# Picking table rows inside the edge loop of a graph layer: from three tiles of one group to one tile of most groups

## The reference

```
row, col = src, dst
h   = relu(bn(concat(x[row], edge_attr) @ W1 + b1))      # 53125 x 128, bn over all edges
agg = segment_sum(h, col) / max(count(col), 1)           # 3125 x 128
h2  = relu(bn(concat(x, agg) @ W2 + b2))                 # 3125 x 256, bn over all nodes
out = layernorm(x + relu(h2 @ Wl + bl))                  # 3125 x 128
```

## Time and profile before

| | us |
|---|---|
| time, three runs | 586.23, 587.31, 763.84 (median 587.31) |
| profiled execution, its own time | 585.97 |
| its span, first to last instruction | 584.2 |
| PE busy | 527.9 (90%) |
| PE weight loads busy | 464.9 (80%) |
| DVE busy | 509.0 (87%) |
| ACT busy | 425.3 (73%) |
| POOL busy | 362.0 (62%) |

### The profile page before, as it was taken

One profiled execution on the slowest core, in us unless ns is written; L12 is line 12 of the kernel. 1 busy time (PEld: TensorE's weight loads), 2 busy tenths in 40 slices (PEclk: granted clock), 3 DMA queues, 4 the chain that ended last, 5 costly groups with the idle time before them and its releaser, 6 DMA issues.

```text
span 584.2 us, 10621 instructions
## 1 busy us (share of the span) xinstructions
PE 527.9 (90%) x3099; PEld 464.9 (80%) x3099; DVE 509.0 (87%) x719; ACT 425.3 (73%) x850; POOL 362.0 (62%) x464
## 2 busy tenths in 40 slices
PE   3679999999999999999999988898997999999993
PEld 4658878877778878888888877787885999999583
DVE  5796999999999999999999989898986877777787
ACT  2458777887788777888888877678767566666476
POOL 4776777777777777777777777777770333333500
PEclk9789999999999999999999999899999999999997
DMA  7844454455444554444444444354345688775004
GB/s 197 263 142 125 158 161 143 133 162 167 155 140 146 163 166 141 140 145 139 143 145 148 145 150 148 109 148 150 95 121 164 219 252 267 251 253 169 1 1 111
DMA packets 48139, 90.21 MB, mean 154 GB/s; under 512 B 10885, under 2 KB 30260, under 8 KB 48099
## 3 DMA queue, kind: packets, MB, share of 16 engines
q1 hardware_dynamic: 30734, 59.97, 31.2%
q0 software_dynamic: 10912, 22.37, 15.0%
q10 hardware_dynamic: 6453, 7.38, 3.6%
HBM read 66.71 MB, written 22.97 MB: 153 GB/s over the span
## 4 chain that ended last, share of the span: by engine, by line
PE 55%; DVE 20%; issue 8%; POOL 8%; ACT 4%; DMA 3%; DVEq 0%; ACTq 0%; POOLq 0%
PE psT L784 22%; PE psH L923 8%; PE psC L923 8%; POOL res L682 6%; DVE node_hot L1319 6%; PE psH L766 5%; PE psT L847 4%; DVE psX L1334 3%; PE psC L766 2%; DVE res L1306 2%; PE psH L793 1%; DMA res<-ytab,srci 1%; DVE res L1473 1%; POOL res L666 1%; ACT node_rows_turned L1084 1%
## 5 line engine op out<-in xcount | busy, mean ns | idle before, releaser
L682 POOL DMA_INDIRECT res<-ytab,srci x265 | 250.2, 944 | 81.8 <-issue 77.1
L784 PE MATMUL psT<-node_hot,node_table 125*128 125x384 f32 x1250 | 261.9, 358 | 4.5 <-DVE node_hot L1319 3.7
L784 PEld LDWEIGHTS psT<-node_hot,node_table 125*128 125x128 f32 x1250 | 222.3, 191 | 29.5 <-issue 12.5
L1319 DVE TENSOR_TENSOR node_hot<-agg,psC 125x1920 fp32r<-125x1920 int32 x75 | 161.0, 2147 | 0.0
L1094 ACT ACTIVATE node_hot<-agg,nodeid 125x384 fp32r<-125x384 int32 x250 | 131.8, 603 | 8.8 <-PE psT L784 6.6
L1097 ACT ACTIVATE node_hot<-node_hot,ones 125x1920 fp32r<-125x1920 f32 x50 | 95.1, 1902 | 1.6
L1435 DVE TENSOR_TENSOR work<-res,psX 128x512 f32<-128x512 f32 x104 | 70.8, 687 | 20.2 <-PE psH L923 10.1
L707 POOL TENSOR_TENSOR agg<-agg,srci 128x64 f32 x104 | 32.0, 308 | 74.6 <-ACT srci L1161 55.0
L766 PE MATMUL psH<-w1e,work 128*128 128x256 f32 x268 | 70.5, 385 | 6.0 <-DVE res L1304 3.3
L682 POOL DMA_INDIRECT work<-ytab,srci x64 | 60.7, 948 | 23.7 <-issue 16.8
L1334 DVE TENSOR_TENSOR psX<-agg,psX 128x512 f32<-128x512 f32 x103 | 71.1, 690 | 4.4 <-ACT agg L1031 4.3
(11 more groups left out here) (222 smaller groups left out, 534.8 us busy)
## 6 DMA issues: line engine op xcount, KB each, us to landing
work<-in_edge_attr SPq DMA_DIRECT2D x26, 512.0 KB, 3.6
res<-spill SPq DMA_DIRECT2D x25, 512.0 KB, 3.6
spill<-work SPq DMA_DIRECT2D x13, 512.0 KB, 2.8
spill<-res SPq DMA_DIRECT2D x12, 512.0 KB, 2.9
agg<-in_src_rows SPq DMA_DIRECT2D x25, 192.0 KB, 3.9
res<-ytab,srci POOLq DMA_INDIRECT x265, 2.6
res<-h2x_dram SPq DMA_DIRECT2D x10, 312.5 KB
h2x_dram<-agg ACTq DMA_DIRECT2D x12, 250.0 KB
```

Source lines behind the costliest of these rows:

```text
L682: pool.indirect_dma_start(rows[:, j * F:(j + 1) * F], None, ytab, bass.IndirectOffsetOnAxis(ap=srci[:, j, g:g + 1], axis=0)).then_inc(gath ...
L784: last = pe.matmul(rows_at, table[0:PN, part, (t0 + t) * F:(t0 + t + 1) * F], hot_now[0:PN, t, :], start=(n == 0 and t == 0 and part == 0) ...
L1319: dve.tensor_tensor(dve_hot(i, d)[0:PN, :, :], rows[i % 2][0:PN, :].bitcast(I32).unsqueeze(1).broadcast_to([PN, CUT, HOTW]), nodep[:, t0:t ...
```

## The change

Rows are picked with one-hots as weights. For each group one tile (the first) is picked, in all groups from step 1 on except q = 3 of the even steps to 14 and of steps 16, 20 and 24, and the last two groups. The 25 places of a partition are cut into 7 blocks of 4. The one-hot of a block (125 x 128 edges) is the weight, and the four table rows of that block (512 columns) stream through it, for the high and the low part: 14 matmuls a pick, two of them with 128 columns. The result, edges on partitions with four candidate rows each, lies in one of two accumulators `psR` (psC[1] and psT[0]; the product has two left, `psP`). DVE takes the right one with four dependent operations (`take_row`), multiplying each candidate with 0 or 1 from a small table `sel`, into h's place, and then adds the product as for gathered rows. Nothing is turned back.

The one-hots are made by pairs of groups (256 columns): blocks 0 to 3 by ACT, 4 to 6 by DVE, in three sets of buffers. The comparison is with a key, the source number less its place within its block; DVE works keys and `sel` out before step 0, SP writes the keys to DRAM (`key_dram`) and spreads a step's four tiles from there. load_ea(2) comes before that on SP. PE's order in a step is, for each q: pick, then the product of the next group, with x_product after q = 0 and counts after q = 1. W2's product on x is written with x read in stretches of neighbours, and ACT's copy reorders it.

```diff
-        HOTW = PICKED * P
-        CUT = 5
+        HOTW = U * P
+        HALF = HOTW // 2
...
-        psP = [psH[0], psH[1], psC[1]]
+        psP = [psH[0], psH[1]]
+        psR = [psC[1], psT[0]]
...
+        def picked(i, q):
+            if i < NODE0 or (i == NI - 1 and q >= 2):
+                return False
+            return not (q == U - 1 and i % (2 if i <= len(XSTEPS) else 4) == 0)
+        PICKS = [(i, q) for i in range(NI) for q in range(U) if picked(i, q)]
...
             def load_rows(i):
                 if i >= NODE0 + 2:
-                    sp.wait_ge(hot_by_dve, len(DVE_CUTS) * (i - NODE0 - 1))
-                    sp.wait_ge(dist_ready, NT // NP * len(ACT_CUTS) * (i - NODE0 - 1))
-                sp.dma_start(rows[i % 2].bitcast(I32), src_rows[i - NODE0, :].partition_broadcast(P)
+                    sp.wait_ge(hot_by_dve, pairs_through(i - 2))
+                    sp.wait_ge(hot_by_act, pairs_through(i - 2))
+                sp.dma_start(rows[i % 2], key_dram[U * i:U * (i + 1), :].rearrange("q e -> (q e)").partition_broadcast(P)
                              ).then_inc(rows_in[i % 2], 16)
             load_ea(1, 1)
+            load_ea(2, 0)
+            sp.wait_ge(s_keyed, 1)
+            sp.dma_start(key_dram, keyq[:, NG:KW]).then_inc(s_keyd, 16)
+            sp.wait_ge(s_keyd, 16)
             for i in range(NODE0, NODE0 + 2):
                 load_rows(i)
-            load_ea(2, 0)
             for i in range(NI - 3):
...
                 rows = slot(i, i % 2, q)
-                for j in range(node_tiles(i) if q == NODEQ else 0, TILES):
+                for j in range(1 if picked(i, q) else 0, TILES):
...
+            def pick(i, q):
+                n = pick_number(i, q)
+                a = q // 2
+                if n == 0 or PICKS[n - 1][0] != i or PICKS[n - 1][1] // 2 != a:
+                    pe.wait_ge(hot_by_dve, PAIRS.index((i, a)) + 1)
+                    pe.wait_ge(hot_by_act, PAIRS.index((i, a)) + 1)
+                if n >= len(psR):
+                    pe.wait_ge(row_part, RAD * (n - len(psR) + 1))
+                hot_now = pair_set(i, a)
+                e0 = (q - 2 * a) * P
+                for t in range(NC1):
+                    w = min(RAD, NT - RAD * t) * F
                     for part in range(2):
-                        last = pe.matmul(rows_at, table[0:PN, part, (t0 + t) * F:(t0 + t + 1) * F],
-                                         hot_now[0:PN, t, :], start=(n == 0 and t == 0 and part == 0),
-                                         stop=(n == NP - 1 and t == CUT - 1 and part == 1))
-                last.then_inc(nhot_used, 1)
-            def rows_back(i):
-                pe.wait_ge(rows_kept, i - NODE0 + 1)
-                for j in range(node_tiles(i)):
-                    last = pe.matmul(psP[(U * i + NODEQ) % len(psP)][:, j * F:(j + 1) * F], rowst_sb[:, j * P:(j + 1) * P], ident[:, :],
-                                     start=False, stop=(j == node_tiles(i) - 1))
-                last.then_inc(rows_added, 1)
+                        last = pe.matmul(psR[n % len(psR)][:, 0:w], hot_now[0:PN, t, e0:e0 + P],
+                                         table[0:PN, part, RAD * t * F:RAD * t * F + w],
+                                         start=(t == 0 and part == 0), stop=(t == NC1 - 1 and part == 1))
+                last.then_inc(rows_picked, 1)
...
-                pe.matmul(psT[1][:, 0:n * NT].rearrange("o (p t) -> o p t", t=NT), w2x[:, h * P:(h + 1) * P],
-                          xtv[:, :, k:k + n].rearrange("f t p -> f p t"), start=True, stop=True).then_inc(x_ps, 1)
+                pe.matmul(psT[1][:, 0:n * NT].rearrange("o (t p) -> o t p", t=NT), w2x[:, h * P:(h + 1) * P],
+                          xtv[:, :, k:k + n], start=True, stop=True).then_inc(x_ps, 1)
...
-                product(i, par, nth, 1)
-                if i in NODES:
-                    pick(i, 0)
-                if i <= len(XSTEPS):
-                    x_product(i - 1)
-                if i in NODES:
-                    pick(i, 1)
-                product(i, par, nth, 2)
-                if i in NODES:
-                    pick(i, 2)
-                    pick(i, 3)
-                product(i, par, nth, 3)
-                counts(i, par)
-                if i in NODES:
-                    pick(i, 4)
-                    rows_back(i)
-                if i + 1 < NI:
-                    product(i + 1, 1 - par, (i + 1) // 2 + 1, 0)
+                for q in range(U):
+                    if picked(i, q):
+                        pick(i, q)
+                    if q == 0 and i <= len(XSTEPS):
+                        x_product(i - 1)
+                    if q + 1 < U:
+                        product(i, par, nth, q + 1)
+                    elif i + 1 < NI:
+                        product(i + 1, 1 - par, (i + 1) // 2 + 1, 0)
+                    if q == 1:
+                        counts(i, par)
...
+                if (i, a) not in PAIRS:
+                    return
+                act.wait_ge(rows_in[i % 2], 16 * ((i - NODE0) // 2 + 1))
+                if picks_before(i, a):
+                    act.wait_ge(rows_picked, picks_before(i, a))
+                c0, c1 = pair_columns(i, a)
+                t0, t1 = ACT_CUT
+                at = pair_set(i, a)
+                for t in range(t0, t1):
+                    act.activation(at[0:PN, t, c0:c1], rows[i % 2][0:PN, a * HALF + c0:a * HALF + c1], ACT.Abs,
+                                   bias=nodeid[0:PN, t:t + 1], scale=-1.0).then_inc(dist_ready, 1)
+                act.wait_ge(dist_ready, (t1 - t0) * (PAIRS.index((i, a)) + 1))
+                act.activation(at[0:PN, t0:t1, c0:c1], at[0:PN, t0:t1, c0:c1], ACT.Relu, bias=ones[0:PN, :], scale=-1.0
                                ).then_inc(hot_by_act, 1)
-            node_hot(NODE0, 0)
-            x_product_out(0)
-            node_hot(NODE0, 1)
+            for a in range(2):
+                node_hot(NODE0, a)
             for i in range(1, NI - 1):
                 squares(i, 0)
+                if i <= len(XSTEPS):
+                    x_product_out(i - 1)
+                node_hot(i + 1, 0)
+                squares(i, 1)
                 place_counts(i)
...
+            def take_row(i, par, q, r):
+                n = pick_number(i, q)
+                if r == 0:
+                    dve.wait_ge(gathered[par][q], gathers_through(i, q))
+                    dve.wait_ge(rows_picked, n + 1)
+                else:
+                    dve.wait_ge(row_part, RAD * n + r)
+                own = slot(i, par, q)[:, 0:F]
+                ps = psR[n % len(psR)][:, r * F:(r + 1) * F]
+                mine = sel[:, r, U * i + q:U * i + q + 1]
+                if r == 0:
+                    dve.tensor_scalar(own, ps, mine, None, ALU.mult).then_inc(row_part, 1)
+                else:
+                    dve.scalar_tensor_tensor(out=own, in0=ps, scalar=mine, in1=own, op0=ALU.mult, op1=ALU.add
+                                             ).then_inc(row_part, 1)
...
+                dve.wait_ge(rows_in[i % 2], 16 * ((i - NODE0) // 2 + 1))
+                if picks_before(i, a):
+                    dve.wait_ge(rows_picked, picks_before(i, a))
+                c0, c1 = pair_columns(i, a)
+                t0, t1 = DVE_CUT
+                dve.tensor_tensor(pair_set(i, a)[0:PN, t0:t1, c0:c1],
+                                  rows[i % 2][0:PN, a * HALF + c0:a * HALF + c1].unsqueeze(1).broadcast_to(
+                                      [PN, t1 - t0, c1 - c0]),
+                                  nodep[:, t0:t1].unsqueeze(2).broadcast_to([PN, t1 - t0, c1 - c0]), ALU.is_equal
                                   ).then_inc(hot_by_dve, 1)
...
+            def onehots_between(i, q):
+                if q == 0:
+                    onehots(i + 1)
+                elif q == 1:
+                    node_onehots(i + 1, 0)
+                elif q == 3:
+                    node_onehots(i + 1, 1)
             def edge_step(i, par, nth):
                 for q in range(U):
-                    make_h(i, par, nth, q)
-                    sum_h(i, par, q)
-                    if U * i + q:
+                    if picked(i, q):
+                        take_row(i, par, q, 0)
+                        onehots_between(i, q)
+                        take_row(i, par, q, 1)
                         sum_sq(U * i + q - 1)
-                    if q == 0:
-                        onehots(i + 1)
-                        if i == NODE0:
-                            node_onehots(i, 2)
-                    elif i >= NODE0:
-                        node_onehots(i + 1, q - 1)
+                        take_row(i, par, q, 2)
+                        take_row(i, par, q, 3)
+                        make_h(i, par, nth, q)
+                        sum_h(i, par, q)
+                    else:
+                        make_h(i, par, nth, q)
...
+            dve.wait_ge(s_keys, 16)
```

(44 more changed lines are left out.)

129 lines of the change are left out of this document (52 added, 77 removed).

## The result

The changed kernel takes **612.2 us** (median of 4 runs, 611.7 to 613.2) against 586.8 for the kernel before: ratio **1.045** (95% interval 1.043 to 1.047). The forecast was 576.5 us, faster, with a range to 600: the sign was wrong, and the time lies outside the range. The profiled execution took 611.72 us.

A forecast was written before the change was run, and what follows sets the result against it. GpSimd's 329 gathers at 1.249 us were taken to bound the edge loop. Forecast: 23.08 + 394.7 (316 gathers) + 9 (start) + 6 x 0.2 (pairs) + about 2 = 430.0, plus 146.4 behind it: 576.4 us, range 569 to 600.

The forecast's parts named there:

- The place of trouble: On PE behind pick(i,2): two products with no pick between, the second, product(i+1,0), waiting for h of (i,2).
- 16.2 + 13.3 + 1.9: PE's time for a pair of edge-loop steps: four-pick step, three-pick step and wait, 31.4 us against GpSimd's 31.2 for 25 gathers.
- PE's work: PE's matmuls in a pair of edge-loop steps: 16.2 us with four picks and 13.3 with three.
- The stand: PE's wait in a three-pick step: VectorE's chain from pick to h takes 2.7 us, one product lies beside it, leaving 1.9.
- a sign of being wrong: Listed under what would show the forecast wrong: a granted clock below the 1.00 of the three stretches before.
- three-pick step: Edge-loop step in which three groups pick a tile: 13 gathers (16.2 us) on GpSimd, 13.3 us on PE plus a wait.
- saved 16.2 us: GpSimd's gain in the edge loop: 13 fewer gathers, if it stands still no longer than before.
- four-pick step: Edge-loop step in which all four groups pick: PE 16.2 us (15.3 in steps 15 to 24), VectorE 15.0, GpSimd 15.0.
- Picks at the columns' own speed: Rival on PE's picks: fixed part hidden behind 512 columns, a pick 2.7 us, 573 us in all; chance 0.2.
- PE takes GpSimd's place: Rival: 128-column matmuls cost full fp32 price, a pick 3.2 us, a pair on PE 33.7, 601 us in all; chance 0.18.
- The handshake costs more than its parts: Rival: in every group's loop of pick, takes, h and product, takes cost 0.07 and signals 0.1 more; 584 to 590; chance 0.22.

The follow-up runs named there:

- experiment 4: The kernel before with only W2's product on x reading neighbours and ScalarE's copy reordering: 584.6 us, 0.998 of the kernel before.
- experiment 5: The changed kernel with two of the four takes of every picked group left out: 585.7 us, 0.999 of the kernel before.
- experiment 3: The changed kernel with ten small fp32 matmuls, result unread, where PE would wait in three-pick steps: 601.0 us, 1.026 of the kernel before.
- the best version: The changed kernel with a pick where PE stood, picks from step 2, VectorE's one-hots later, step 2's built during step 1: 581.4 us, 0.991 of the kernel before.

## Why the prediction was wrong

**What held.** The bound of before is GpSimd (experiment 4). 316 gathers stay. The prices of matmuls were close: the pick 2.90 to 2.95 (forecast 2.86), W2's product 0.92 (0.86). Inside a pick the trace has the 512-column matmuls 0.227 us apart, as forecast, and the 128-column ones 0.057, so these are not at fp32 price. The place of trouble was named too: the second of two products behind pick(i,2), which waits for h(i,2).

The Trainium skill's rule for an isolated matmul, in "TensorE: Matmul & The Clock Gate", section "Back-to-back issue gap", gives an estimate of 2.7 for a pick; the chain's 2.90 to 2.95 speak against it.

**The step that failed** is the pair of steps on PE, "16.2 + 13.3 + 1.9", set at 31.4 against GpSimd's 31.2. It measured 34.36, and three of its terms were off:
- PE's work: 29.5 forecast, 30.6 measured (experiment 5). Each pick cost 0.04 to 0.09 more than forecast, each product behind a pick 0.05 more: small, but some fourteen times a pair.
- The stand: 1.9 forecast (its own terms give 1.83), 2.15 measured. A dependent take starts 0.38 after the one before it (row below), not 0.33. The 2.15 is idle time by the profile, which shows the product ahead of it as 1.08 long; reckoned with the forecast's 0.86 the stand is 2.4 and PE's work 30.3.
- The clock: nothing forecast. The windows of before all have 1.00, and the text listed a lower clock only as a sign of being wrong. It costs 34.36 - 32.70 = 1.7 us in a pair with a fall, more than either of the others, and experiment 3 gets 11.2 us back by keeping PE busy alone. The Trainium skill, in "TensorE: Matmul & The Clock Gate", section "What's actually happening", has the array slow by default, "and activity releases the throttle". Experiment 3 agrees: with the stands filled the granted clock is 1.00 from 100 to 400 us, and 0.97 without.

The takes behind the last pick of a three-pick step, in the timeline of VectorE (changed kernel):

```profile
178.66 0.35 DVE L1326 TENSOR_SCALAR work<-psT,table_choice 128x128 f32<-128x128 f32 x1
179.04 0.35 DVE L1328 SCALAR_TENSOR_TENSOR work<-psT,table_choice,work 128x128 f32<-128x128 f32 x1
179.31 0.69 DVE L1356 TENSOR_TENSOR psX<-agg,psX 128x512 f32<-128x512 f32 x1
179.90 0.73 DVE L1328 SCALAR_TENSOR_TENSOR work<-psT,table_choice,work 128x128 f32<-128x128 f32 x2
180.77 0.69 DVE L1312 TENSOR_TENSOR work<-psH,work 128x512 f32<-128x512 f32 x1
```

**What the sum made of it.** A pair over 31.2 takes the bound away from GpSimd, and then its saved 16.2 us are worth nothing: it waits 42.5 us for h instead. From 78.51 to 282.54, six pairs, are 204.0 us where 188.4 were forecast: 15.6. From there to 380.88, four four-pick steps and two of three, are 98.3 where GpSimd's gathers are 92.4: 5.9. Here it is not only the clock: the four-pick step from 340.49 to 356.99 takes 16.50 us at a granted clock of 1.00, with PE busy 16.10 and VectorE 15.48, where the forecast had 15.3 and 15.0. The first h of step 1 is ready at 53.7 instead of 50.9, 2.8 late: above all since the first pick ran 4.66 us behind its stand of 9.51, where 2.86 had been put (granted clock 0.66 from 45.10 to 49.80). That leaves 10 of the 34.6 us by which ScalarE's end misses the forecast's 433.5. Some 7.6 of them come behind GpSimd's last gather: ScalarE ends 11.1 us after it (468.13 - 456.99), where the forecast had 3.5. The column sums run there at a granted clock of 0.52 (458.50 to 465.00), and at 1.00 in the kernel before. The other 2.7 lie in steps 1, 2 and 21 to 25. I did not take these apart by experiment. In the forecast a stand was an amount of time that adds to a step. In the run it also made the following work dearer, and it came at the same place of every pair, where PE had nothing else queued.

**The rivals.** *Picks at the columns' own speed* fell by the chain's rows. *PE takes GpSimd's place* had the right engine, sign and nearly the size (601), for a reason that is not there: no narrow matmul was dear. *The handshake costs more than its parts* had the reason nearest to the truth, takes 0.35 long and 0.38 apart, and priced it at 584 to 590, since it left the clock out. The kernel comes to lie near this once the stand is filled with a pick (591.9), and in it once the stand is shortened (585.7). In the best version the change gives 0.9%. PE and VectorE are busy 97% and 94% of the stretch from 100 to 400 us there, and GpSimd starts 239 of 240 possible gathers.

**What stays open.** Three of the nine stands, those of 2.30 to 2.40 us such as that at 216.24, have no fall in the product and pick behind them. They are longer than the six with a fall, and no run here says what sets them apart.

## What to carry to other kernels

When a change brings two engines to within a per cent or two of each other, forecast the places where one must wait for another with nothing else queued, and not only the sums: here the order of a pick and a product on PE was worth 20 us, and half of the picks' matmuls 26. Price a stand of PE twice: once as time, and once as the work behind it at half clock. Before an experiment leaves work out, try putting other work, useful or not, into the gap.

## What was not expected of the hardware

- The granted clock fell behind six stands of 2.15 to 2.22 us, and not behind three of 2.30 to 2.40. Behind those of 1.27 us in the experiment with two takes the products kept their length of 1.10.
- Matmuls whose result nobody reads made the kernel 11 us faster.
- A product behind a pick takes 0.91 us, and behind W2's product on x 0.86, for the same four passes.
